# A graph layer in one program: the node phase reordered, the edge tables moved into it, 22 of 202 gather groups staged in DRAM

## What is computed

```python
xn = layernorm(x)
# branch 1: edge attention over a graph
f = xn @ W_n                                  # (N, 8, 32)
el, er = einsum(f, attn_l), einsum(f, attn_r)  # (N, 8, 4)
e = leaky((el[src] + er[dst] + e_pro @ attn_m) . mask / 3)
rst = segment_sum(f[src] * segment_softmax(e, dst), dst)
# branch 2: linear attention
q, k, v = split(xn @ Wqkv)
q = softmax(q, within a head) * 32**-0.5
k = softmax(k, over all nodes)
mix = layernorm((k^T v applied to q) @ Wout) * gamma
x = x + rst + mix
# branch 3: a mixture of 8 experts of three layers on layernorm(x)
return x + ffn(layernorm(x))
```

## Time and profile before

| | us |
|---|---|
| median of 3 executions (lowest, highest) | 3594.44 (3593.63, 3603.38) |
| the profiled execution: its own time | 3594.56 |
| the profiled execution: span of the trace | 3592.9 |
| node phase, about | 0 to 461 |
| edge tables, to the first instruction of the edge phase | 461 to 516 |
| edge phase | 516 to about 2632 |
| FFN phase | 2632 to 3592.9 |

### The profile page before, as it was taken

The page is one execution under the profiler, slowest core; times in us unless marked ns, Lnnn a source line. Parts: engine busy times, 40 slices in busy tenths (PEclk is TensorE's granted clock), DMA queues, the critical chain, the costliest instruction groups (busy, mean ns, idle before and its releaser), DMA issues. The chain is left out here.

```text
span 3592.9 us, 79682 instructions
## 1 busy us (share of the span) xinstructions
PE 3076.7 (86%) x21675; PEld 2485.6 (69%) x21676; DVE 2724.5 (76%) x5311; ACT 1675.6 (47%) x5730; POOL 1648.0 (46%) x1798
## 2 busy tenths in 40 slices
PE   7988617888888888888888888888859999999999
PEld 4666405676776767677666767676638888888888
DVE  4667726888888888888888888888858776777776
ACT  3433203555555555555555555555533333333333
POOL 2210227777777777777777777777500000000000
PEclk9987858999999999999999999999969999999999
DMA  2200336666666666666666666666421000100000
GB/s 77 78 33 18 105 119 181 180 184 178 182 180 184 181 178 182 176 181 176 182 181 181 182 179 183 182 181 181 126 77 57 19 19 20 37 19 20 19 10 13
DMA packets 346109, 434.87 MB, mean 121 GB/s; under 512 B 156833, under 2 KB 254144, under 8 KB 345838
## 3 DMA queue, kind: packets, MB, share of 16 engines
q0 software_dynamic: 85616, 259.65, 26.9%
q1 hardware_dynamic: 260222, 172.47, 16.5%
HBM read 374.16 MB, written 57.73 MB: 120 GB/s over the span
## 5 line engine op out<-in xcount | busy, mean ns | idle before, releaser
L846 POOL DMA_INDIRECT gat<-scratch_table,idx x1616 | 1553.3, 961 | 508.2 <-issue 481.9
L1162 PE MATMUL ps_s<-msg,oh 128*128 128x272 f32 x4000 | 1013.9, 402 | 27.7 <-ACT tmp L888 18.7
L1162 PEld LDWEIGHTS ps_s<-msg,oh 128*128 128x128 f32 x4000 | 734.0, 191 | 165.1 <-ACT tmp L888 24.7
L1014 DVE TENSOR_TENSOR msg<-gat,ps_m 128x2048 f32<-128x2048 f32 x250 | 560.6, 2284 | 91.5 <-issue 91.5
L1418 ACT ACTIVATE h<-ps_h,fsh,fsc 128x512 f32<-128x512 f32 (+1 forms) x416 | 290.8, 750 | 565.0 <-PE ps_h L1603 565.0
L897 ACT ACTIVATE acc<-acc,sc 128x33 f32<-128x33 f32 x2000 | 459.0, 340 | 162.8 <-DVE acc L1005 162.8
L877 ACT CAST oh<-ps_o 128x1024 f32<-128x1024 bf16 x250 | 259.2, 1037 | 397.7 <-PE ps_o L1102 395.1
L1383 POOL DMA_DIRECT2D out<-y x12 | 9.1, 762 | 923.9 <-DVE y L1558 923.9
L888 ACT ACTIVATE tmp<-ps_s,sc 128x33 f32<-128x33 f32 x2000 | 384.4, 304 | 17.2
L1139 PE MATMUL ps_e<-ident,e 128*16 128x128 f32 x1000 | 149.7, 299 | 258.6 <-DVE e L973 258.6
L1458 DVE CAST h_hi<-h 128x1024 fp32r<-128x1024 f32 (+1 forms) x208 | 137.3, 660 | 239.7 <-ACT h L1418 239.5
(11 more groups left out here) (194 smaller groups left out, 5375.9 us busy)
## 6 DMA issues: line engine op xcount, KB each, us to landing
d16r<-scratch_dst SPq DMA_DIRECT2D x250, 256.0 KB
scratch_acc<-acc SPq DMA_DIRECT2D x250, 136.0 KB
gat<-scratch_table,idx POOLq DMA_INDIRECT x1616
a<-in_a SPq DMA_DIRECT2D x250, 64.0 KB
scratch_table<-trow POOLq DMA_DIRECT2D x49, 144.0 KB, 2.0
am<-scratch_acc SPq DMA_DIRECT2D x12, 544.0 KB, 4.1
xin<-in_x SPq DMA_DIRECT2D x49, 128.0 KB, 2.0
xre<-in_x SPq DMA_DIRECT2D x49, 128.0 KB, 2.0
```

What stands on the lines that cost most here:

```text
L846: pool.indirect_dma_start(out=gat[:, s, c, :], out_offset=None, in_=scr["table_rows"], in_offset=bass.IndirectOffsetOnAxis(ap=idx[:, g * C ...
L1014: dve.tensor_tensor(m4[:, :, :, 0:DH], gat[:, row_of(at), :, 0:D].rearrange("p a c (h d) -> p (a c) h d", h=H), ps_p.rearrange("p (c j h) ...
L1162: last = pe.matmul(ps_s[j][:, 0:SUMS], oh[:, s, j, c, :], msg[:, 2 * (s % 2) + j, c, :], start=(c == 0), stop=(c == C - 1), skip_group_che ...
```

## The change

- `tiles` can write all steps out (`unrolled=True`, used for TensorE's loops) and put a piece in after step 4 (`between`).
- Loop 1 now makes only the table row and the `er` part; x turned is kept for all tiles in `xq`. The edge tables' loads are issued behind the loads of x tiles 0 and 1, and VectorE's work on them stands after its step 4. SP stores them after the loads of x, behind three late weight loads and a load of indices.
- A second loop makes q, k and v of the kept tiles. ScalarE waits ahead of it until all edge tables are stored (their buffers share memory with `ktile`). VectorE's work on q (maxima, subtraction, sums) moves into this loop, with the running maximum of k.
- A third loop subtracts the maximum from k, scales q in place and accumulates the context; the sums of k come from an added column of v.
- The split of `er` is done for all tiles at once, in five instructions around the making of `mixw`, and stored in one DMA of SP, ahead of the second loads of x. SP also takes over the stores of the fourth loop from GpSimd.
- GpSimd, once the table is stored, gathers 22 groups (every seventh: 6, 13, ... 153) through two staging buffers into the DRAM tensor `ahead`: 8 groups ahead of the maximum over partitions and 14 behind it. The edge phase has 7 slots in place of 6, and GpSimd fetches those 22 groups with one plain DMA each.

The diff, cut to its core (declarations, renamed semaphores and lines that only move are left out):

```diff
-GSLOTS = 6
+GSLOTS = 7
+PRE = 22
+PRE_FIRST = 8
...
@@ sync
+                if isinstance(t, int) and t == 1:
+                    for dst, name in ((d_em, "dst_em"), (dn_em, "dst_next_em"), (d_lin, "dst_lin"),
+                                      (dp_lin, "dst_prev_lin")):
+                        sp.dma_start(dst[:, :], io[name].rearrange("(p n) -> p n", p=P)).then_inc(dst_in, 16)
...
             tiles(sp, (load_x, 0))
+            for dst, src in late:
+                sp.dma_start(dst, src).then_inc(late_in, 16)
+            sp.dma_start(pidx[:, :].rearrange("p (i c) -> p i c", c=C),
...
+            sp.wait_ge(derived, 1)
+            sp.dma_start(scr["dm"].rearrange("g p c -> (g p c)").rearrange("(q n) -> q n", q=P),
+                         dm[:, :]).then_inc(stored, 16)
...
+            sp.wait_ge(er_step, 5)
+            sp.dma_start(scr["er"].rearrange("t p n -> p t n"), er3[:, :, :]).then_inc(stored, 16)
+            sp.wait_ge(kmaxb_ok, 1)
...
-            tiles(sp, (reload, 0))
+            def store_mix(t, s):
+                sp.wait_ge(mixf_ok, t + 1)
+                sp.dma_start(scr["xmix"][row_of(t), :, :].rearrange("a p n -> (a p) n"),
+                             mixf[:, s, :]).then_inc(mix_out[s], 16)
+            tiles(sp, (reload, 0), (store_mix, 2))
+            sp.wait_ge(stored, 16 * (STORED + 1))
...
@@ gpsimd
             tiles(pool, (store_table, 0))
+            pool.wait_ge(pidx_in, 16)
+            pool.wait_ge(table_out[0], 16 * ((NT + 1) // 2))
+            pool.wait_ge(table_out[1], 16 * (NT // 2))
+
+            def store_ahead(i):
+                pool.wait_ge(staged[i % 2], 16 * C * (i // 2 + 1))
+                pool.dma_start(scr["ahead"][i], stage[:, i % 2, :, :].rearrange("p c n -> p (c n)")) \
+                    .then_inc(ahead_out[i % 2], 16)
+
+            def gather_ahead(i):
+                if i >= 2:
+                    pool.wait_ge(ahead_out[i % 2], 16 * (i // 2))
+                for c in range(C):
+                    pool.indirect_dma_start(
+                        out=stage[:, i % 2, c, :], out_offset=None, in_=scr["table_rows"],
+                        in_offset=bass.IndirectOffsetOnAxis(ap=pidx[:, i * C + c:i * C + c + 1], axis=0),
+                    ).then_inc(staged[i % 2], 16)
+                    if c == C // 2 - 1 and i > 0:
+                        store_ahead(i - 1)
+
+            for i in range(PRE_FIRST):
+                gather_ahead(i)
             pool.wait_ge(kmax_ok, NT)
             pool.partition_all_reduce(kmaxb[:, :], kmax[:, :], P, RMAX).then_inc(kmaxb_ok, 1)
+            for i in range(PRE_FIRST, PRE):
+                gather_ahead(i)
+            store_ahead(PRE - 1)
+            pool.wait_ge(ahead_out[0], 16 * ((PRE + 1) // 2))
+            pool.wait_ge(ahead_out[1], 16 * (PRE // 2))
...
@@ scalar
+            tiles(act, (spread, 0), (turn, 1), (keep_row, 2))
+            act.wait_ge(stored, 16 * STORED)
+            act.wait_ge(ident_ok, 2)
+            def keep(t, s):
+                act.wait_ge(qkv, t + 1)
+                settle(act)
+                act.copy(flat(ktile, t), ps_qk[s][:, D:2 * D]).then_inc(kept, 1)
+                act.copy(flat(xq, t), ps_qk[s][:, 0:D]).then_inc(kept, 1)
+                act.copy(vtile[:, row_of(t), 0:D].rearrange("p a n -> p (a n)"), ps_v[s][:, 0:D]).then_inc(kept, 1)
...
+            tiles(act, (keep, 0), (exp_q, 1))
+            tiles(act, (exp_k, 0))
...
@@ vector
-            tiles(dve, (measure, 0), (norm, 1), (split, 3))
+            tiles(dve, (measure, 0), (norm, 1), between=edge_tables)
+            tiles(dve, (maxima, 0), (sum_q, 2))
...
+            tiles(dve, (shift, 0), (soften, 1))
+            dve.wait_ge(ksub, NT)
+            split_er(0)
             dve.wait_ge(ctx_mm, NT)
...
+            split_er(3)
+            split_er(4)
+            dve.wait_ge(late_in, 16 * 3)
...
-            tiles(dve, (soften, 0), (finish, 3), (measure_out, 2))
+            tiles(dve, (finish, 1), (measure_out, 0))
...
@@ tensor
-            tiles(pe, (turn, 0), (project, 1))
+            tiles(pe, (turn, 0), (project, 1), unrolled=True)
+            pe.wait_ge(late_in, 16 * 3)
+            def project_qkv(t, s):
+                if later(t):
+                    pe.wait_ge(kept, (t - 1) * 3)
...
+            tiles(pe, (project_qkv, 0), unrolled=True)
...
@@ phase_edges, gpsimd
+            def ahead(g):
+                return g % GSLOTS == GSLOTS - 1 and g // GSLOTS < PRE
...
+                if ahead(g):
+                    pool.dma_start(gat[:, GSLOTS - 1, :, :].rearrange("p c n -> p (c n)"),
+                                   scr["ahead"][g // GSLOTS]).then_inc(gathered[GSLOTS - 1], 16)
+                    landed(g - 1)
+                else:
+                    for c in range(C):
+                        gather(g, c)
...
-    phase_edge_tables(nc, io, scr)
```

More of the change, by code:

```diff
@@ L84, in later, with tiles @@
     return not (isinstance(t, int) and t < 2)
-def tiles(eng, *stages):
+def tiles(eng, *stages, between=None, unrolled=False):
     def step(t, s):
@@ L98, in tiles @@
         step(t, t % 2)
-    with eng.Fori(0, (NT - 5) // 2) as k:
-        for u in (0, 1):
-            step(k * 2 + (5 + u), (5 + u) % 2)
+    if between:
+        between()
+    if unrolled:
+        for t in range(5, NT):
+            step(t, t % 2)
+    else:
+        with eng.Fori(0, (NT - 5) // 2) as k:
+            for u in (0, 1):
+                step(k * 2 + (5 + u), (5 + u) % 2)
     for t in range(NT, NT + max(lag for _, lag in stages)):
@@ L155, in phase_nodes @@
         weights_in = sem("n_weights_in")
+        late_in = sem("n_late_in")
         blocks_in = sem("n_blocks_in")
@@ L314, in keep @@
-                act.copy(vtile[:, row_of(t), :].rearrange("p a n -> p (a n)"),
-                         ps_v[s][:, 0:D]).then_inc(kept, 1)
-            tiles(act, (spread, 0), (turn, 1), (keep, 2))
-            def exp_kq(t, s):
+                    act.wait_ge(table_out[s], (t - s) * 8)
+                act.copy(trow[:, s, :], ps_ft[s][:, 0:ROW]).then_inc(trow_ok, 1)
+                act.copy(flat(er_f, t), ps_ft[s][:, ROW:ROW + HT]).then_inc(trow_ok, 1)
+            tiles(act, (spread, 0), (turn, 1), (keep_row, 2))
@@ L475, in turn, with part @@
                 if later(t):
-                    pe.wait_ge(xnT_ok, t - 1)
+                    pe.wait_ge(turn_ok, t - 1)
                 for k in range(KD):
                     last = pe.transpose(ps_tr[s][:, k, :], xn[:, s, k * P:k * P + P], ident[:, :])
-                last.then_inc(xnT_ps, 1)
+                last.then_inc(turn_ps, 1)
+            def part(t, at, k):
+                return t[:, row_of(at), k * P:k * P + P].rearrange("p a n -> p (a n)")
             def project(t, s):
-                pe.wait_ge(xnT_ok, t + 1)
+                pe.wait_ge(turn_ok, t + 1)
+                if later(t):
+                    pe.wait_ge(trow_ok, (t - 1) * 2)
+                settle(pe)
+                for k in range(KD):
+                    last = pe.matmul(ps_ft[s][:, 0:D + 2 * HT], part(xq, t, k), wcat[:, k, :],
+                                     start=(k == 0), stop=(k == KD - 1))
+                last.then_inc(proj, 1)
@@ L489, in project @@
                 for k in range(KD):
-                    pe.matmul(ps_qk[s][:, :], xnT[:, s, k, :], wqkv[:, k, 0:2 * D],
-                              start=(k == 0), stop=(k == KD - 1))
-                for k in range(KD):
-                    last = pe.matmul(ps_v[s][:, 0:D], xnT[:, s, k, :], wqkv[:, k, 2 * D:3 * D],
+                    last = pe.matmul(ps_v[s][:, 0:D], part(xq, t, k), wqkv[:, k, 2 * D:3 * D],
                                      start=(k == 0), stop=(k == KD - 1))
-                last.then_inc(proj, 1)
@@ L658, in phase_edges @@
+            tiles(pe, (turn_q, 0), (attend, 1), unrolled=True)
 def phase_edges(nc, io, scr):
@@ L849, in gather @@
                 ).then_inc(gathered[s], 16)
+            def ahead(g):
+                return g % GSLOTS == GSLOTS - 1 and g // GSLOTS < PRE
             def landed(g):
-                pool.wait_ge(gathered[g % GSLOTS], 16 * C * (g // GSLOTS + 1))
+                parts = sum(1 if ahead(f) else C for f in range(g % GSLOTS, g + 1, GSLOTS))
+                pool.wait_ge(gathered[g % GSLOTS], 16 * parts)
                 pool.nop(nofuse=True).then_inc(ready, 1)
@@ L860, in _ @@
                 settle(pool)
-                for c in range(C):
-                    gather(g, c)
-                    if c == C // 2 - 1 and g > 0:
-                        landed(g - 1)
+                if ahead(g):
+                    pool.dma_start(gat[:, GSLOTS - 1, :, :].rearrange("p c n -> p (c n)"),
+                                   scr["ahead"][g // GSLOTS]).then_inc(gathered[GSLOTS - 1], 16)
+                    landed(g - 1)
+                else:
+                    for c in range(C):
+                        gather(g, c)
+                        if c == C // 2 - 1 and g > 0:
```

(1 more changed line is left out.)

457 lines of the change are left out of this document (197 added, 260 removed).

## The result

The changed kernel takes 3650.6 us (median of 4, 3649.8 to 3651.8), the kernel before 3596.0 beside it: a ratio of **1.0153** (95% interval 1.0138 to 1.0168), 54.6 us slower. I had forecast 24 us, with 3652 as the upper end. The profiled execution took 3650.95, its span is 3649.3, 56.4 more than before.

What follows compares the result with a forecast made beforehand. It took the VectorE and TensorE chain to bound the edge phase, GpSimd close behind. Edge phase 26 us later, 2 us gained in it: +24 on 3594.56 gives 3618 us, range 3578 to 3652.

Steps and rivals of the forecast that it cites:

- The edge phase: Edge steps: the chain of VectorE and TensorE is the bound, so 22 groups less save nothing; 2 us quicker, -8 to +6.
- The first rival: Edge steps: the gathers bound them after all, gain 68 us, net -42, 3552 us; chance 0.12.
- the others: Node phase: tail hidden and last loop at 1.75, 3585 to 3595, chance 0.20; something else ends it, 3637, together 0.16.
- The tail of the columns: Ahead of the q, k, v loop: ScalarE waits for the stores, SP's issues to 194.4 plus 21.9, 216.3; between 194 and 222.
- q, k, v loop: Second node loop: TensorE sets it at 2.59 us a tile, to 342.7; bounds 126 to 140 us.
- context loop: Third node loop: 1.2 us a tile and 4 us for a slow start, to 414; bounds 57 to 85 us.
- mixw: Behind the context loop: 6.5 us as before plus 4 for splits of `er`, to 424.5.
- The maximum over partitions: Between q, k, v and context loops, on GpSimd: 5.53 us idle and 1.08 busy, to 349.3; 1.1 to 6.6.
- the last loop: Fourth node loop: 2.1 us a tile with gathers in the DMA engines, to 535; 1.75 (86 us) to 2.5 (122 us).
- The `er` store ahead of the reload: Ahead of the last loop: `er` store before the second x load makes first results about 7 us late, 432; bounds 2 to 12.
- The start of the edge phase: Ahead of the first edge step: needs groups 0 to 5, all still gathered; no change in time was given.
- The barrier: End of the node phase: landing of the last result and barrier stay, 7 us behind 535, so the edge phase begins at 542.

Runs made afterwards that it cites:

- e1_no_staging: Changed kernel without the 22 staged groups, the edge phase gathering all 202 itself: 3613.0 us, ratio 1.0056 to the kernel before.
- f1_gathers_only: Changed kernel with the 176 staged gathers but no stores to `ahead`, the edge phase gathering all 202 groups: 3630.3 us, ratio 1.0117 to the kernel before.
- f3_all_rows: Changed kernel without staging, with the added iota, x by three DMAs, second x and results in v's memory, columns as rows: 3499.6 us, ratio 0.9748 to before.
- e2_iota: Changed kernel with one more iota of one column at the end of GpSimd's node list: 3637.2 us, ratio 1.0125 to the kernel before.
- f2_xbulk: Changed kernel with x loaded by three DMAs into the memory of v in place of 49 loads: 3570.4 us, ratio 0.9937 to the kernel before.
- e4_vlast: Changed kernel, staging kept, second x (two DMAs) and results in the memory of v, `er` store behind those loads: 3618.3 us, ratio 1.0079 to the kernel before.
- f4_all_staged: Same edits as `f3_all_rows` on the changed kernel, but with the 22 staged groups kept: 3509.8 us, ratio 0.9772 to the kernel before.

## Why the prediction was half right

- **The edge phase: right.** It rested on TensorE hardly waiting for gathered rows against a GpSimd that was never free. Steps of 16.43 to 16.46 us with all groups gathered (`e1_no_staging`, `f1_gathers_only`, `f3_all_rows`) and of 16.41 to 16.51 with 22 of them fetched show it, and GpSimd's waits for slots grew by 167 us. The first rival (gathers bound the steps, 3552) falls. So do the others: the tail wasn't hidden, and the 14 groups behind the maximum took 11.4 us each (349.7 to 509.5), so GpSimd was done before the last result.
- **The tail of the columns: right in kind, and near in its end by luck.** ScalarE did wait for it, 22.4 us. But SP was through its issues at 207.5, not 194.4: the last load of x was issued 5.6 us later than forecast (a tile took 3.59 us on average from tile 5 on, not 3.45), and the 19 DMAs behind it took 16.0 us, not 8.8, since the store of `dm` held SP for 4.70 us at its issue, where I had counted 0.46. From the last issue it was then only 15.4 us, where I took 21.9 from the table phase. Nearly 13 late and 6.5 short leave the 6.4 of the table.
- **q, k, v loop, context loop, mixw**: within 1 to 3 us each, all shorter. The maximum over partitions was 5.3 shorter: the 5.53 us of the earlier trace rows is the exchange of GpSimd's code, which in the changed kernel ran at 306.5, in its wait for the maximum.
- **The step that failed is the last loop.** I took 2.1 us a tile with gathers in the DMA engines, from loads that landed after 3 to 4 us. Measured are 2.1 behind the staging and 2.87 beside it (28 tiles in 80.4 us), 2.5 on average, my upper bound. With the gathers alone it was 2.16 (`f1_gathers_only`), near my 2.1; what I left out is the stores to `ahead`. They stood in the GpSimd part as 0.54 us of issue, and not as 1.2 MB that SP's store of tile t-2 shares its DMA engines with. The loop is 20.3 us of the 32.3 missed, and 17.4 of them are these stores.
- **The `er` store ahead of the reload**: 16.4 us to the first result in place of 7.5, though the wait itself (10.4) is within the bounds of 2 to 12. 3.5 us are the last split behind `mixw`, which I had counted ahead of it; the load behind the store then took 12.3 us to land. The staging is half of the 8.9 missed: without it the load took 7.9 us and the whole 12.0.
- **The start of the edge phase was no term of the sum**, with 7.7 us. The trace of before held the price (11 us at GpSimd's iota of the table stretch, behind a maximum over partitions), and the change took its cover away. I had put the phase down as unchanged because its code was.
- **The barrier was 4.8 us shorter.** I had carried over 7 us from before as the landing of the last result; there they ended with GpSimd's DRAIN (467.9), which in the changed kernel is over at 526.2.

The missed terms are +6.4, +8.9, +20.3 and +7.7, less 15.5 from the parts that were shorter; with 1.6 us that the edge steps didn't give and 2.9 behind them it is 32.3 on top of the 24, 56.3 of the 56.4.

The Trainium skill (Trainium Kernel Development and Optimization, Key Constraints) has the DMAs of SP, ScalarE and GpSimd on the same 16 DMA engines. `e1_no_staging` and `f1_gathers_only` agree (the loop of SP's transfers is 29 and 17 us shorter without GpSimd's, or without its stores), and so do GpSimd's stores that took 10 to 22 us beside SP's columns. The 512-byte rule of the Trainium skill (DMA: Bandwidth & Descriptors, Specifications), that transfers below that size don't reach line rate, agrees with the columns: 1,280 elements of 4 bytes, 5 KB, took 21.5 us from the first issue to the start of the loop, and as rows of 512 bytes 4.6 us. The size alone doesn't set the price: 128 rows of 192 bytes landed in 1.8 us.

## What to carry to other kernels

Work moved onto an idle engine isn't free when its transfers are large: look for every ring of two buffers whose store has to land, and price it with the new bytes in flight, or give it memory in which it needn't wait. Relieving an engine that is always busy gains nothing while its consumers don't wait for it, and the consumer's row tells that. Before two phases are merged, list what the idle stretch between them covered, GpSimd's exchange of code and the tails of small stores among it, and ask when GpSimd's list ends, since the barrier waits for its DRAIN.

## What the runs showed of the hardware

- On GpSimd, going from an iota to the maximum over partitions cost 5.5 us of idle time, and going back 7.0 (`e2_iota`), 9.6 (changed kernel) and 11 us (before), each behind a MODIFY_POOL_CONFIG record. It doesn't wait for what the instruction itself waits for (the record stands at 306.5, the maximum's input was ready at 348.2), so it can be hidden by issuing a cheap instruction of the kind early. The Trainium skill (GPSIMD Engine Reference, Instruction dispatch) puts the load of fresh code at about 6 us: the maximum's agrees, the iota's is longer by these rows.
- 1,280 stored elements of 4 bytes held up the table's stores for about 30 us: four of these, of 144 KB each, landed after 10 to 22 us, with a median of 2.1 for all 49 (`f2_xbulk`).
- GpSimd's DRAIN at the end of the node phase took 4.2 us in the kernel before, 7.8 in the changed kernel and in `e4_vlast`, and ended 7.8 us behind its last iota in `f4_all_staged` (426.2 to 434.1). It costs only where GpSimd is the last engine at the barrier: 7.3 us in the last two.
- x in 3 DMAs in place of 49 that wait for a buffer cut VectorE's waits for it from 121.6 us to 21.9 and brought the last table row from 199.8 to 151.7 (`f2_xbulk`), and to 121.4 with the columns as rows (`f3_all_rows`).
